# Two attention stages of a Perceiver kernel: maxima of a key block taken in four-row groups at the head, and mask and maxima of the latent attention added by products in the banks

## The chip, the cores and the metric

The kernel runs on one core of one Trainium2 chip. The metric is the device time of one execution in microseconds (us), the median of several runs. PE is the matrix engine (TensorE), DVE the vector engine, ACT the scalar engine, POOL GpSimd, SP the engine whose queue issues the transfers; a PSUM bank holds 512 float32 columns in 128 partitions.

## The reference

A two-layer model over 16 batches of 64 latent rows, width 256, with 1601 context rows a batch. Layer 0 has a cross-attention with relative embeddings, a latent (low-rank) causal self-attention and a mixture of experts; layer 1 a masked cross-attention, a delta rule and a quantised feed-forward part. The change lies in the first two. Cut to what matters:

```python
x = x + xattn(layernorm(x), ctx, ctx, ...)      # first cross-attention
#   q, k, v = x Wq + bq, ctx Wk + bk, ctx Wv + bv     16 heads of 16; 64 queries, 1601 keys
#   attn = softmax((q k^T + q rel_k[clip(k - q, -2, 2)]) / 4)
#   out  = (attn v + attn rel_v[...]) Wo + bo
x = x + latent(layernorm(x), ...)               # latent attention
#   lat = layernorm(x W_dkv) * gamma + beta ; k, v = lat W_uk, lat W_uv ; q = x W_q
#   scores = rope(q) rope(k)^T / 4, -inf above the diagonal  (64 x 64, 16 heads)
#   out = softmax(scores) v W_o
x = x + moe(...) ; x = x + xattn(..., mask) ; x = x + delta_rule(...) ; x = x + fp4_mlp(...)
```

A softmax may subtract any number near the row's maximum; both stages subtract a maximum that is found in a pass of its own.

## The kernel before

Everything lies in SBUF between stages; each engine's instructions are written out by hand in the order in which it runs them, with semaphores between engines. `cross_attention` (L185) serves both cross-attentions: the first has `rel` and no mask, the second `mask` and no `rel`. `latent_attention` (from L1052) comes between.

**Cross-attention.** A body runs once for a batch b and does two things beside each other: it attends batch b, and it prepares the keys and maxima of batch b + 1 ("ahead"). There are 17 bodies; 15 of them, b = 0 to 14, do both, in pairs (p = 0, 1), most of them in a hardware loop.

The head of a body on PE: products for the relative embeddings (L922); `key_block` 1 of the next batch (L757, block 0 was made at the end of the last body); `denominators` (L854); `key_block` 2; the transposes of the negated maxima of batch b (L946); `key_block` 3; in even batches the `output` product (L860); `project_values(0)` (L868); then `scores(0)`, which waits until DVE has multiplied the transposed maxima by `pmask` into `nmb` (L685), since each score bank begins with a product of `nmb` with ones (L897).

The loop over chunks of 128 keys, two chunks c, c + 1 a step, c = 0, 2 to 12: `scores(c)` into banks 1 to 4 (L897, L905), `maximum(SCORED[c])`, `attend_values` of the two chunks before (L885), `maximum(VALUED[c])`, `project_values(c + 2)` (L868), `maximum(PROJECTED[c])`. ACT takes the exponentials of a step in one pass (L556), DVE copies the projected values (L698).

The maxima of the next batch are approximate, from bfloat16 copies of queries and keys (`qbf`, `kbf`). A unit is `maximum(u)`: two products of 32 rows into banks 5 and 6 (L843), and one reduction of both by DVE (L675); the next unit waits for that reduction (`max_read`). Units of key block 0 have four more products for the relative embeddings (L848). `ALL` lists 4 key blocks x 4 units. `HEADED` names groups of four products into banks 1 to 4 with one reduction over four banks (`headed(j)`, L809 on PE with products on L820, L666 on DVE with the reduction on L669); the second cross-attention has three of them at the head, the first has none. `LOOPED` is what is left for the loop.

POOL, for the next batch: copies for the relative products (`qs`), then behind the reduction `ds_done` a table (`scores_table`, L418), two products into `Dxb` (L459), and the casts of the four key blocks to bfloat16 (`keys`, L435), each when ACT has written the block (L490); then four products with `kmask` (L473) for the batch attended.

DVE at the head: denominators (`rec` L654, `oN` L656), `nmb` (L685), in even batches the addition of the output to X (L664), the first value copy.

**Latent attention.** After projections, rotation and transposes a loop over 16 batches. Before the change: `scores(b)` on PE writes 8 groups of 64 x 64 scores into banks 0 to 3 (L1309). DVE's `shift(b)` adds the mask while it copies them to SBUF (`sc`, three buffers; L1219), reduces the maxima (L1225) and subtracts them (L1226). ACT takes exponentials in place (L1155). DVE's `normalise(b)` sums (L1231), takes reciprocals (L1234) and multiplies (L1235). PE transposes the result (L1329), ACT copies it (L1163), PE multiplies by the values (L1344), ACT copies that (L1169), and every second batch PE multiplies by `wo` (L1318) and DVE adds to X (L1240). The scores run up to three batches ahead.

## Time and profile before

| | us |
|---|---|
| median of 3 runs | 2667.76 |
| lowest, highest | 2666.96, 2674.25 |
| the profiled execution | 2666.93 |
| its span, first to last instruction | 2665.1 |

| engine | busy us in the span | share |
|---|---|---|
| PE | 2457.0 | 92% |
| PE weight loads (beside PE) | 1769.6 | 66% |
| DVE | 1432.5 | 54% |
| ACT | 975.5 | 37% |
| POOL | 583.1 | 22% |

The mean granted clock of PE is 0.958 of 2.4 GHz. The first cross-attention's bodies that do both things fill most of the first 814 us, the latent attention ends at 977 us. Shares are means over stages with different limits, so the two stages are read by themselves. A view by line groups instructions by engine, line and tile: busy time, mean duration in ns, and the idle time of the engine ahead of them with what ended it. The timeline gives instructions in order of time, equal neighbours merged (x count); in brackets the idle time before, and what released it. The view by stretch gives the stretch's length and then the busy us of PE, PE's loads, DVE, ACT and POOL.

### The profile page before, as it was taken

To read this page: it belongs to the slowest core of one execution; us is meant where nothing else is said; L and a number is where in the kernel's file an instruction comes from. 1 tells how busy PE (TensorE), PEld (TensorE's weight loads), DVE (VectorE), ACT (ScalarE), POOL (GpSimd) and SP (SyncE) were. 2 spreads that over 40 slices of the span, in tenths; PEclk is the share of its full clock that TensorE was granted. 3 is DMA by queue.
4 is the path that set the end of the run, shared out by engine and by line. 5 is a ranking of instruction groups with operands and counts; after the bars stand their busy time and mean duration, and the time that the engine had idled before them with its cause. 6 is when DMAs were issued, how large, how long until landed. Compare 5 with 4: busy or idle time off the path is not lost. (4 is left out here: it accounts for less than half of the span.)

```text
span 2665.1 us, 91180 instructions
## 1 busy us (share of the span) xinstructions
PE 2457.0 (92%) x41601; PEld 1769.6 (66%) x41601; DVE 1432.5 (54%) x2340; ACT 975.5 (37%) x1286; POOL 583.1 (22%) x504
## 2 busy tenths in 40 slices
PE   7999999999998878979999999999879988998798
PEld 4776776776676655736676767676567777777466
DVE  4454454454453763365555454554556666666468
ACT  2333333333333331224444444443434433332223
POOL 2424433432441203231111111211011111111000
PEclk8999999999999659989999999999899999999899
DMA  2111111111010422121111111111100000000200
GB/s 96 33 39 33 33 39 33 28 38 39 27 39 9 182 82 65 56 80 33 45 34 45 40 39 39 39 39 47 55 2 4 4 3 3 4 3 4 83 1 16
DMA packets 56728, 102.30 MB, mean 38 GB/s; under 512 B 10272, under 2 KB 49024, under 8 KB 55024
## 3 DMA queue, kind: packets, MB, share of 16 engines
q1 hardware_dynamic: 54448, 91.35, 11.1%
q8 instruction: 332, 5.44, 0.8%
q0 software_dynamic: 1904, 5.15, 0.5%
q14 instruction: 44, 0.36, 0.0%
HBM read 90.30 MB, written 9.21 MB: 37 GB/s over the span
## 5 line engine op out<-in xcount | busy, mean ns | idle before, releaser
L675 DVE TENSOR_REDUCE x_mx<-banks 128x2 f32<-128x800 f32 (+1 forms) x422 | 416.5, 990 | 385.6 <-PE banks L843 268.1
L868 PE MATMUL banks<-x_wv,x_cT 128*128 128x256 f32 (+1 forms) x1664 | 421.3, 395 | 5.1 <-DVE x_nmb L685 5.1
L757 PE MATMUL banks<-x_cT,x_wk 128*128 128x400 f32 (+1 forms) x1024 | 381.8, 515 | 7.2 <-DMA x_cT<-in_ctx 5.7
L868 PEld LDWEIGHTS banks<-x_wv,x_cT 128*128 128x128 f32 (+1 forms) x1664 | 297.8, 188 | 70.1 <-issue 11.0
L556 ACT ACTIVATE x_PT<-banks 128x2048 f32<-128x2048 f32 (+1 forms) x112 | 196.6, 1755 | 357.9 <-PE banks L905 357.9
L558 ACT ACTIVATE x_PT<-banks,x_kbs 128x1024 f32<-128x1024 f32 (+1 forms) x208 | 221.1, 1110 | 233.1 <-PE banks L905 233.1
L757 PEld LDWEIGHTS banks<-x_cT,x_wk 128*128 128x128 f32 x1024 | 187.9, 192 | 137.5 <-issue 23.3
L905 PE MATMUL banks<-x_qbd,x_kT 32*128 32x128 f32 x6656 | 246.9, 273 | 0.0
L905 PEld LDWEIGHTS banks<-x_qbd,x_kT 32*128 32x128 f32 x6656 | 242.6, 183 | 3.6
L432 POOL TENSOR_TENSOR x_kbf<-x_kT,x_mb 128x400 bf16<-128x400 f32 (+1 forms) x128 | 122.7, 961 | 556.8 <-ACT x_kT L490 556.6
L885 PE MATMUL banks<-x_PT,x_V 128*32 128x64 f32 x13312 | 233.3, 221 | 1.1 <-ACT x_PT L556 0.3
L885 PEld LDWEIGHTS banks<-x_PT,x_V 128*32 128x32 f32 x13312 | 196.6, 110 | 51.4 <-issue 48.0
L698 DVE COPY x_V<-banks 128x512 f32<-128x512 f32 (+1 forms) x224 | 144.5, 645 | 128.0 <-PE banks L868 128.0
L473 POOL TENSOR_TENSOR x_Ej<-x_PT,x_kmask 128x1024 f32<-128x1024 f32 x64 | 148.9, 2361 | 128.8 <-ACT x_PT L556 128.8
L843 PE MATMUL banks<-x_kbf,x_qbf 32*128 32x400 bf16 (+1 forms) x844 | 143.6, 339 | 12.9 <-DVE x_mx L675 3.2
L490 ACT ACTIVATE x_kT<-banks,x_bk 128x400 f32<-128x400 f32 (+1 forms) x128 | 76.0, 594 | 151.6 <-PE banks L757 151.6
L2330 PE MATMUL banks<-d_KQ,d_KB 64*64 64x64 f32 x3584 | 124.2, 220 | 7.6 <-ACT d_KB L1999 3.5
L490 ACT ACTIVATE x_kT<-banks,x_kshift 128x400 f32<-128x400 f32 (+1 forms) x128 | 76.0, 594 | 144.6 <-PE banks L757 144.6
L2330 PEld LDWEIGHTS banks<-d_KQ,d_KB 64*64 64x64 f32 x3584 | 112.6, 134 | 23.3 <-issue 23.3
L2006 ACT ACTIVATE d_Y<-banks 128x512 f32<-128x512 f32 x96 | 57.3, 597 | 177.4 <-PE banks L2330 177.4
L843 PEld LDWEIGHTS banks<-x_kbf,x_qbf 32*128 32x128 bf16 x844 | 40.5, 91 | 113.5 <-issue 63.2
L669 DVE TENSOR_REDUCE x_mx<-banks 128x4 f32<-128x1604 f32 (+1 forms) x45 | 82.1, 1825 | 58.7 <-PE banks L820 58.7
(406 smaller groups left out, 3696.2 us busy)
## 6 DMA issues: line engine op xcount, KB each, us to landing
x_cT<-in_ctx SPq DMA_DIRECT2D x96, 400.0 KB, 3.7
x_cT<-in_ctx SPq DMA_DIRECT2D x32, 401.0 KB, 3.7
e_up<-in_mo_up SPq DMA_DIRECT2D x9, 512.0 KB, 15.6
e_down<-in_mo_down SPq DMA_DIRECT2D x9, 512.0 KB, 16.4
x_mrow<-in_mask_row SPq DMA_DIRECT2D x1, 3202.0 KB, 14.3
t_w<-in_db_w SPq DMA_DIRECT2D x3, 1024.0 KB, 8.4
e_rows<-in_c_unfilled SPq DMA_DIRECT2D x1, 2967.0 KB, 13.1
e_xg<-e_rows SPq DMA_DIRECT2D x23, 129.0 KB, 2.0
```

Of the source, the lines that this page charges most:

```text
L473: pool.tensor_tensor(Ej[:, j, :].rearrange("p (h q) -> p h q", h=H), PT[:, 0, 0, :].rearrange("p (h q) -> p h q", h=H), kmask[:, j, None, ...
L490: act.activation(kT[:, 1 - p, gg, KB0[k]:KB0[k] + KBS[k]], PJ[pb][:, 0:KBS[k]], ACT.Identity, bias=kshift[:, gg, b:b + 1] if mask else bk[ ...
L556: act.activation(out, got, ACT.Exp, scale=HD ** -0.5, bias=0.0).then_inc(exp_done, n2)
L558: act.activation(out[:, :, a], got[:, :, a], ACT.Exp, scale=HD ** -0.5, bias=kbs[0:CHK[c], p, c + a:c + a + 1]).then_inc(exp_done, 1)
L675: dve.reduce_max(mx[:, H0[k]:H0[k] + 3:2, kb], g.PS[:, first:first + 2, 0:KBS[kb]], AXX).then_inc(max_read, 1)
L698: dve.tensor_copy(V[0:CHK[c], c % 6:c % 6 + n2, :, 0:HD], PJ[pb][0:CHK[c], 0:D * n2].rearrange("p (a h d) -> p a h d", a=n2, h=H)).then_in ...
L757: last = pe.matmul(PJ[pb][:, 0:KBS[k]], wk[:, c, gg, :], cT[:, (p + 1) % 2, c, KB0[k]:KB0[k] + KBS[k]], start=c == 0, stop=c == KC - 1)
L843: last = pe.matmul(g.P[first + x][:, 0:KBS[kb]], qbf[rows(r), gg, :, :].rearrange("p i q -> p (i q)"), kbf[rows(r), gg, keys], start=True, ...
L868: last = pe.matmul(PJ[pb][0:CHK[c + k], D * k:D * k + D], cT[:, p, cc, 128 * (c + k):128 * (c + k) + CHK[c + k]], wv[:, cc, :], start=cc = ...
L885: last = pe.matmul(OT[r:r + 32, S * (h // 4):S * (h // 4) + S], V[0:CHK[c], c % 6, h, :], PT[0:CHK[c], c // 2 % NPT, c % 2, S * h:S * h + ...
L905: last = pe.matmul(SC[r][0:CHK[c + a], at:at + HPT * S], kT[rows(r), p, gg, 128 * (c + a):128 * (c + a) + CHK[c + a]], qbd[rows(r), p, gg, ...
L2330: last = pe.matmul(out, lhs(E[e], hp), rhs(E[e], hp), start=k > 0 or start, stop=True, skip_group_check=True)
```

## The change

Two edits that share no code.

**First cross-attention.** `HEADED` of the first cross-attention becomes the two groups of key block 1. On PE the first comes behind `key_block` 2 and the second behind `key_block` 3; `BEHIND` holds these places for both cross-attentions, and the second one's stay as they were. DVE reduces the first group behind the denominators and ahead of `nmb`, the second behind `nmb`. POOL casts key block 0 ahead of its wait for `ds_done`, block 1 behind the small table, and blocks 2 and 3 behind the products into `Dxb`, as before. The twelve units left go to new places: all `SCORED` and `PROJECTED` slots from c = 2 on (and 0 for the first), and of the `VALUED` slots only c = 4.

**Latent attention.** A score bank now begins with a product of a bfloat16 identity with the bfloat16 mask, the scores accumulate on it, DVE reduces the negated maximum straight from the banks into a bfloat16 tile (`nmb`, two buffers), and a second set of identity products (`shift(b)`, now on PE) adds it in the bank. ACT takes the exponentials from the banks into `sc`. The two DVE passes of the mask's addition and of the subtraction are gone. The scores of a batch wait for the exponentials of the batch before (`ex_done`) instead of for the copy. The order on PE is new: shift of b + 1, scores of b + 2, an output, values of b - 1, transposes of b. The addition of the output to X comes one batch later. Two small copies on DVE make the identity and the mask bfloat16, ahead of the scaling of the latents by gamma.

```diff
-        HEADED = [(0, 0), (0, 1), (1, 0)] if mask else []
+        HEADED = [(0, 0), (0, 1), (1, 0)] if mask else [(1, 0), (1, 1)]
+        BEHIND = {0: [0], 1: [1], "shift": [2]} if mask else {2: [0], 3: [1]}
+        EARLY = 2 if mask else 0
...
+        else:
+            SCORED = {2: 1, 4: 3, 6: 6, 8: 8, 10: 10}
+            VALUED = {4: 4}
+            PROJECTED = {0: 0, 2: 2, 4: 5, 6: 7, 8: 9, 10: 11}
...
-            def keys(bank, plan, p, b):
-                for k in range(NKB):
+            def keys(bank, plan, p, b, blocks=range(NKB)):
+                for k in blocks:
...
+                        if attend:
+                            keys(bank, plan, p, b + 1, (0,))
                         pool.wait_ge(ds_done, b + 2)
                         if attend:
                             scores_table(b, p)
+                            keys(bank, plan, p, b + 1, (1,))
...
                     if attend:
-                        keys(bank, plan, p, b + 1)
+                        keys(bank, plan, p, b + 1, range(2 if rel else 0, NKB))
...
-                for j in range(ahead_of - 1):
+                for j in range(EARLY) if ahead_of else ():
                     headed(j)
                 if tail and attend:
                     denominators()
+                if ahead_of and not mask:
+                    headed(0)
...
-                    placed = range(NHD) if attend else ()
...
+                    for k in range(NKB - 1) if attend else ():
+                        if k and b:
+                            key_block(bank, plan, i, p, k)
+                        for j in BEHIND.get(k, ()):
+                            headed(j)
+                        if k == 1 and b:
                             denominators()
...
-                    if ahead and NHD:
-                        headed(2)
+                    for j in BEHIND.get("shift", ()) if ahead else ():
+                        headed(j)
                     if ahead and b:
                         key_block(bank, plan, i, p, NKB - 1)
+                    for j in BEHIND.get(NKB - 1, ()) if ahead else ():
+                        headed(j)
...
             def exponentials(b):
-                act.wait_ge(sub_done, b + 1)
-                act.activation(sc[:, b % 3, :, :], sc[:, b % 3, :, :], ACT.Exp, scale=HD ** -0.5).then_inc(ex_done, 1)
+                act.wait_ge(shifted, b + 1)
+                if b >= 3:
+                    act.wait_ge(tr_full, b - 2)
+                act.activation(sc[:, b % 3, :, :].rearrange("p (c r) k -> p r c k", c=KC),
+                               g.PS[:, 0:4, 0:2 * S].rearrange("p r (c k) -> p r c k", c=KC), ACT.Exp, scale=HD ** -0.5)\
+                   .then_inc(ex_done, 1)
...
+            dve.tensor_copy(identb[:, :], g.ident[:, :]).then_inc(masks_done, 1)
+            dve.tensor_copy(causalb[:, :], causal[:, :]).then_inc(masks_done, 1)
...
-                dve.tensor_tensor(x.rearrange("p (c r) k -> p c r k", c=KC),
-                                  g.PS[:, 0:4, 0:2 * S].rearrange("p r (c k) -> p c r k", c=KC),
-                                  causal[:, None, None, :].to_broadcast([128, KC, 4, S]), ALU.add).then_inc(s_read, 1)
...
-                done(dve.reduce_max(m[:, :], x, AXX))
-                dve.tensor_tensor(x, x, m[:, :, None].to_broadcast([128, 8, S]), ALU.subtract).then_inc(sub_done, 1)
+                if b >= 2:
+                    dve.wait_ge(shifted, b - 1)
+                dve.tensor_reduce(nmb[:, b % 2, :].rearrange("p (c r) -> p c r", c=KC),
+                                  g.PS[:, 0:4, 0:2 * S].rearrange("p r (c k) -> p c r k", c=KC), AXX, ALU.max, negate=True)\
+                   .then_inc(max_done, 1)
...
-            shift(0)
-            shift(1)
+            maximum(0)
             for b in range(B):
+                if b + 1 < B:
+                    maximum(b + 1)
                 normalise(b)
-                if b + 2 < B:
-                    shift(b + 2)
-                if b >= 2 and b % 2 == 0:
-                    add_output(b // 2 - 1)
+                if b >= 4 and b % 2 == 0:
+                    add_output(b // 2 - 2)
+            add_output(B // 2 - 2)
             add_output(B // 2 - 1)
...
             def scores(b):
                 if b >= 1:
-                    pe.wait_ge(s_read, b)
+                    pe.wait_ge(ex_done, b)
+                for r in range(4):
+                    pe.matmul(g.P[r][:, 0:2 * S], identb[:, :], causalb[:, None, :].to_broadcast([128, KC, S]),
+                              start=True, stop=False, skip_group_check=True)
...
+            def shift(b):
+                pe.wait_ge(max_done, b + 1)
+                for r in range(4):
+                    last = pe.matmul(g.P[r][:, 0:2 * S], identb[:, :],
+                                     nmb[:, b % 2, r:8:4, None].to_broadcast([128, KC, S]), start=False, stop=True, skip_group_check=True)
+                last.then_inc(shifted, 1)
...
+            for b in range(B + 1):
+                if b + 1 < B:
+                    shift(b + 1)
+                if b + 2 < B:
+                    scores(b + 2)
+                if b >= 3 and b % 2 == 1:
+                    output((b - 1) // 2 - 1)
+                if b >= 1:
+                    attend(b - 1)
+                if b < B:
+                    turned(b)
```

## Rows read from the trace of the kernel before

**Rows 1.** Stretches: start:end, us, busy us (instructions) by engine, TensorE clock, DMA

```profile
65.50:814.00 748.50, 737.58 (x12749) 525.40 (x12748) 369.60 (x465) 257.54 (x232) 280.37 (x191) 1.00 0.12 34
902.00:977.00 75.00, 54.62 (x608) 39.77 (x608) 58.93 (x104) 23.89 (x49) 0.00 (x0) 0.57 0.00 1
```

**Rows 2.** Timeline, latent loop: two additions of the output to X

```profile
944.12 0.42 DVE L1240 TENSOR_TENSOR X<-X,banks 128x256 f32<-128x256 f32 x1 [0.86 <-PE banks L1318]
952.62 0.42 DVE L1240 TENSOR_TENSOR X<-X,banks 128x256 f32<-128x256 f32 x1 [0.86 <-PE banks L1318]
```

**Rows 3.** Busy time by stretch, the last stretch before the clock rises

```profile
952.00:954.00 2.00, 2.00 (x34) 1.36 (x32) 1.31 (x4) 0.42 (x1) 0.00 (x0) 0.51 0.00 0
```

**Rows 4.** Timeline, first cross-attention: start us, us, engine, line, operation

```profile
439.99 1.10 PE L885 MATMUL banks<-x_PT,x_V 128*32 128x64 f32 x64
441.57 1.99 PE L868 MATMUL banks<-x_wv,x_cT 128*128 128x256 f32 x8
```

**Rows 5.** Timeline, second cross-attention, the same step

```profile
1441.14 1.10 PE L885 MATMUL banks<-x_PT,x_V 128*32 128x64 f32 x64
1442.17 1.99 PE L868 MATMUL banks<-x_wv,x_cT 128*128 128x256 f32 x8
```

**Rows 6.** Timeline, first cross-attention, the step of chunk 10

```profile
400.26 1.88 ACT L556 ACTIVATE x_PT<-banks 128x2048 f32<-128x2048 f32 x1 [3.25 <-PE banks L905]
403.01 0.09 PEld L843 LDWEIGHTS banks<-x_kbf,x_qbf 32*128 32x128 bf16 x2 [0.53 <-DVE x_mx L675]
```

**Rows 7.** Lines of PE, first cross-attention: busy us, mean ns | idle

```profile
L848 PE MATMUL banks<-x_rmaskb,x_Dxb 128*128 128x66 bf16 x240 | 17.7, 196 | 0.0
```

**Rows 8.** Timeline, head of a batch, second cross-attention

```profile
1421.92 0.35 PE L820 MATMUL banks<-x_kbf,x_qbf 32*128 32x400 bf16 x4
1422.20 2.95 PE L757 MATMUL banks<-x_cT,x_wk 128*128 128x400 f32 x8
1422.57 1.82 DVE L669 TENSOR_REDUCE x_mx<-banks 128x4 f32<-128x1600 f32 x1
```

**Rows 9.** Timeline, head of an odd batch, first cross-attention

```profile
413.89 3.76 POOL L459 TENSOR_TENSOR x_Dxb<-x_Ds,x_idq 128x1024 bf16<-128x1024 f32 x2
413.95 0.60 ACT L490 ACTIVATE x_kT<-banks,x_bk 128x400 f32<-128x400 f32 x1 [0.75 <-PE banks L757]
416.17 1.76 DVE L656 TENSOR_TENSOR x_oN<-x_oT,x_rec 128x256 f32<-128x256 f32 x1
416.96 0.42 PE L946 MATMUL banks<-ident,x_nm 128*32 128x128 f32 x8
417.86 0.41 DVE L685 TENSOR_TENSOR x_nmb<-banks,x_pmask 128x256 bf16<-128x256 f32 x1
419.77 1.82 PEld L868 LDWEIGHTS banks<-x_wv,x_cT 128*128 128x128 f32 x8
421.93 0.10 PEld L897 LDWEIGHTS banks<-x_nmb,x_ones 32*128 32x128 bf16 x4 [0.33 <-issue]
```

**Rows 10.** Lines of DVE and ACT, loop of the latent attention

```profile
L1219 DVE TENSOR_TENSOR l_sc<-banks,l_causal 128x512 f32<-128x512 f32 x16 | 10.9, 684 | 0.9 <-PE banks L1309 0.9
L1155 ACT ACTIVATE l_sc<-l_sc 128x512 f32<-128x512 f32 x16 | 10.1, 630 | 9.3 <-DVE l_sc L1226 9.3
```

**Rows 11.** Timeline, PE in the latent loop at the lower clock

```profile
949.77 1.11 PE L1329 MATMUL banks<-ident,l_sc 128*128 128x128 f32 x4 [0.84 <-DVE l_sc L1235]
950.67 1.91 PE L1318 MATMUL banks<-l_wo,l_oT 128*128 128x256 f32 x4
952.52 1.13 PE L1309 MATMUL banks<-l_kT,l_qb 32*128 32x64 f32 x16
953.58 0.58 PE L1344 MATMUL banks<-l_PT,l_V 128*32 128x64 f32 x16
```

**Rows 12.** Timeline, PE in the latent loop at the full clock

```profile
955.26 0.67 PE L1309 MATMUL banks<-l_kT,l_qb 32*128 32x64 f32 x16
956.01 0.43 PE L1344 MATMUL banks<-l_PT,l_V 128*32 128x64 f32 x16
```

More of the change, by code:

```diff
@@ L817, in headed @@
                             pe.wait_ge(exp_done, NCH * b)
-                    pe.wait_ge(kbf_done, KP * (NKB * (b + 1) + kb) + gg + 1)
+                    pe.wait_ge(kbf_done, KP * (NKB * (b + 1) + kb) + (gg + 1 if mask else 1))
                     for r in range(RT):
@@ L928, in body @@
                         pe.wait_ge(max_read, units(b + 1))
-                    placed = range(NHD) if attend else ()
-                    if placed:
-                        headed(0)
-                    for k in range(1, NKB - 1) if attend and b else ():
-                        key_block(bank, plan, i, p, k)
-                        if k == 1:
-                            if placed:
-                                headed(1)
+                    for k in range(NKB - 1) if attend else ():
[4 more added lines that the diff above has]
+                        if k == 1 and b:
                             denominators()
-                    if placed and not b:
-                        headed(1)
                 elif attend:
@@ L1309, in scores, with turned @@
                         last = pe.matmul(g.P[r][:, S * c:S * c + S], qb[32 * r:32 * r + 32, c, b, :],
-                                         kT[32 * r:32 * r + 32, c, S * b:S * b + S], start=True, stop=True)
+                                         kT[32 * r:32 * r + 32, c, S * b:S * b + S], start=False, stop=False, skip_group_check=True)
                 last.then_inc(s_full, 1)
-            def output(i):
-                pe.wait_ge(ot_out, 2 * i + 2)
-                if i >= 1:
-                    pe.wait_ge(x_done, i)
-                for j in range(2):
-                    last = pe.matmul(g.P[6][:, 0:D], oT[:, j, :, :].rearrange("p e q -> p (e q)"), wo[:, j, :],
-                                     start=j == 0, stop=j == 1)
-                last.then_inc(wo_full, 1)
-            for b in range(3):
-                scores(b)
-            for b in range(B):
+            def shift(b):
[4 more added lines that the diff above has]
+                last.then_inc(shifted, 1)
+            def turned(b):
                 pe.wait_ge(pn_done, b + 1)
@@ L1331, in _, with attend @@
                 last.then_inc(tr_full, 1)
-                if b >= 2 and b % 2 == 0:
-                    output(b // 2 - 1)
-                if b + 3 < B:
-                    scores(b + 3)
+            def attend(b):
                 pe.wait_ge(pt_out, b + 1)
@@ L1346, in _, with output @@
                 last.then_inc(av_full, 1)
+            def output(i):
+                pe.wait_ge(ot_out, 2 * i + 2)
+                if i >= 1:
+                    pe.wait_ge(x_done, i)
+                for j in range(2):
+                    last = pe.matmul(g.P[6][:, 0:D], oT[:, j, :, :].rearrange("p e q -> p (e q)"), wo[:, j, :],
+                                     start=j == 0, stop=j == 1)
+                last.then_inc(wo_full, 1)
+            pe.wait_ge(masks_done, 2)
+            scores(0)
+            shift(0)
+            scores(1)
+            for b in range(B + 1):
+                if b + 1 < B:
+                    shift(b + 1)
+                if b + 2 < B:
+                    scores(b + 2)
+                if b >= 3 and b % 2 == 1:
+                    output((b - 1) // 2 - 1)
[3 more added lines that the diff above has]
+                    turned(b)
             output(B // 2 - 1)
```

37 lines of the change are left out of this document (16 added, 21 removed).

## Prediction

> **What bounds the kernel now.** I read the busy time by stretch first, since the change touches two stages that have different limits, and then the order of time inside each. In the first cross-attention (65.5 to 814 us) PE is busy 737.58 of 748.50 us at a clock of 1.00, DVE half of it [rows 1]: PE bounds it, and only PE time or PE waits are worth anything there. In the latent attention's loop over batches (902 to 977 us, 75.00 us for 16 batches) DVE is busy 58.93 us and PE 54.62 at a mean clock of 0.57 [rows 1]. The two additions of an output to X stand 8.50 us apart, which is two batches, and DVE waits 0.86 us before each; in the rest of a period it goes from pass to pass [rows 2]. So DVE bounds the loop, 4.25 us a batch, and PE can run at half speed without being late. The clock rises from 1.2 to 2.4 GHz three times in this loop, each time behind a stretch like 952 to 954 us, where PE worked 2.00 of 2.00 us (output, scores and values without a gap) at a clock of 0.51 [rows 3]; the mean of 0.57 says that it soon falls again.
>
> **First cross-attention: the loop over key chunks.** Four of the sixteen two-bank maxima of the next batch leave the loop, in batches 0 to 14, so 15 times. Each step of two chunks had three slots (behind scores, values and projection); the slot behind the values goes in the steps of chunks 2, 6, 8 and 10 and stays only at 4. With that slot, the next projection starts 1.58 us after the values start [rows 4]. The second cross-attention has the same step without the slot, and there it is 1.03 us [rows 5]: 0.55 us less, about half of it product, half PE waiting for the reduction ahead. I take 0.5 for each of the four, as the steps differ a little: 2.0 us. In the step of chunk 10 PE also waits 0.53 us for a reduction ahead of the last unit; with one unit less in front this wait goes, but the scores of chunk 12 then meet the exponentials of chunk 10, 1.88 us from 400.26, so done at 402.14 against scores that now start at 403.02 [rows 6]. At most 0.8 us can leave this step, 0.5 of it is counted: 0.3 more. Against it, the unit behind the scores of chunk 4 is now one of key block 0, with four more products at 0.074 us [rows 7]: 0.3 lost. Sum: 2.0 us gained a batch. DVE has room: it loses four two-bank reductions and gets two four-bank ones of 1.82 us [rows 8].
>
> **First cross-attention: the head.** PE gets two groups of four products. In the second cross-attention such a group takes 0.28 us from its start to the next work [rows 8]: 0.56 us. Whether it waits, for an odd batch: group 0 would start at 416.96, in place of the transposes of the maxima [rows 9]. Its keys come from POOL, which now casts block 1 behind the small table and ahead of the two large products (3.76 us) [rows 9]: ACT ends block 1 at 414.55 [rows 9], and even at the price of one such product, 1.88, the cast is done at 416.43. The large products and the casts of blocks 2 and 3 come later on POOL's queue; they end near 420 and 422, and their first reader stands behind the scores of chunk 0, which start at 421.93. On DVE the four-bank reduction queues ahead of the product with pmask, for which scores(0) waits: from 417.93 (end of the normalisation that began at 416.17) 1.82 us to 419.75, then 0.41 to 420.2 [rows 8, 9]. PE needs that bank for the projection at 419.77 + 0.56 = 420.33, so it is in time by 0.1 us. Group 1 goes out at 420.05, before the projection; its reduction can start at 420.75 (0.65 behind the product, as in rows 8) and ends at 422.6, while PE wants scores(0) at 421.93 + 0.56 = 422.5: 0.1 us of waiting. In an even batch the output product lies between and covers it. Head: 0.56 + 0.1 = 0.66 us. The cover is thin: what DVE is later than this, PE waits. Net 2.0 - 0.66 = 1.34 us a batch, times 15: **20 us gained**.
>
> The normalisation just named reads two SBUF tiles and takes 1.76 us beside POOL's large product, where its size asks 0.4 (0.41 for the equally large product that reads a bank) [rows 9]. The Trainium skill (SBUF — State Buffer, Who interferes with whom) says that such a VectorE instruction and a GpSimd one exclude each other for the whole instruction. The trace agrees: 1.76 us. What it does here is a rival below.
>
> **Latent attention.** Removed on DVE: the mask's addition and the subtraction of the maximum, each 0.68 us; the maximum stays and reads banks [rows 10]. With the addition to X moved one batch back its wait of 0.86 us per two batches goes too [rows 2]: 4.25 - 1.37 - 0.43 = 2.45 us a batch for DVE. It is no longer the bound. Next is a chain through one set of banks: the scores of a batch can't be written before the exponentials of the last have read them. Chain: shift products, exponentials 0.63 [rows 10], mask and scores, maximum 0.68 [rows 10], shift. PE, in order, also runs values, transposes and every second batch the output, and stands idle while ACT reads the banks. Eight new bf16 products of 128 columns a batch: no row has them; at 66 columns four cost 0.30 [rows 7], twice the columns at most 0.59. I take 0.3 at the full clock, as the stored side is the same, and 0.5 at half.
> At 1.2 GHz a batch on PE is shift 0.5, idle 0.85 (the exponentials and the hand-overs around them), mask 0.5, scores 1.06, values 0.65, transposes 0.90, and the output 1.85 more in every second batch [rows 11]: 4.5 or 6.3 us. At 2.4 GHz it is 0.3, 0.85, 0.3, scores 0.75, values 0.43 [rows 12], transposes 0.55 and output 0.95 (half of rows 11, rounded up): 3.2 or 4.15. Batches 0 to 13 hold eight short and six long iterations; what lies around them (first batch, last normalisation, output, addition) I put at 10 us full, 13 at half. All at half: 36 + 38 + 14 = 88 us, 13 more than now; all at full: 25.6 + 24.9 + 10 = 60.5, 14.5 less. Which clock? PE at half would work four fifths of the time and seven eighths around an output, unbroken for five us, more than the stretch behind which it rose [rows 3]; at full its share is about 75 to 80%, between the 98.5% that held 1.00 and the 73% that did not [rows 1]. I let the first iterations, which have no output, run at half, and the rest at full: 6 + 3 x 4.5 + 5.3 + 5 x 3.2 + 5 x 4.15 + 7 = 68.6, or 6 less; with some chance that it is full from the start I take **8 us gained**. The two bf16 copies on DVE ahead of the loop run while PE projects the queries, and cost nothing; without that cover they cost at most two passes of the size in rows 10, 1.4.
>
> The products' price has a rule against it: the Trainium skill (TensorE: Matmul & The Clock Gate, LDWEIGHTS) gives a weight load as columns / 1.2 in ns, an estimated 107 ns for each of these eight. By it four products take 0.43 instead of 0.3, the loop gains 4 us instead of 8, and the time would be 2643. Here a product of rows 7 took 74 ns with its load beside it.
>
> **Sum.** The profiled execution took 2666.93 us (span 2665.1 and 1.8 around it), 0.8 below the median of 2667.76. 2666.9 - 20 - 8 = 2638.9, so 2639.
>
> **Rivals.**
> *Low clock in the latent loop.* PE waits for ACT once a batch, so the clock could fall each time as it does now. Then -20 + 13: 2660. Against it: the waits get shorter than now.
> *Normalisation held twice.* If POOL's two large products, now 1.7 us later, both go ahead of it, DVE's head runs 1.6 us late, and group 1, and behind it scores(0), about 1.2 us: 15 x 1.2 = 18 us of the 20 are gone: 2657. Against it: now it is done at 417.93, 0.3 after the product then running ended (413.89 + 3.76) [rows 9]. By the skill's rule too it waits for one instruction.
> *Reductions in the open (slower).* If DVE reaches both four-bank reductions only when PE stands before scores(0), their 3.64 us replace the 0.66: 1.64 us lost a batch, 25 in all, and with 8 gained elsewhere 2684. It decides against the change from 1.9 us of waiting a batch on (1.34 + 8/15). Against it: the times above, which leave 0.1.
> *It doesn't shorten the steps.* If the slot behind the values hid other PE work, only the head's cost is left: 15 x 0.66 = +10, -8: 2669.
>
> **How the numbers follow.** Forecast 0.70 (2625 to 2652), low clock 0.11, normalisation 0.08, slots that hide 0.06, reductions in the open 0.05. The range to 2657 leaves out the last two and part of the low clock. A measurement here can tell 0.3%, 8 us. Faster by more: 0.70 + 0.08 + a little of the low clock, 0.80; within: 0.14; slower: 0.06.
>
> **What would show it.** Projections 1.0 instead of 1.6 us behind the values in the steps of chunks 6 and 8; DVE's first four-bank reduction ahead of 418 and no wait of PE before scores(0) over 0.3 us; in the latent loop DVE no longer busy throughout, PE's longest wait for the exponentials, clock above 0.8. A clock under 0.7 there, or PE waiting over 1 us for a reduction in the head, makes it wrong.

## The result, and the profile after

The changed kernel takes 2651.0 us (median of 7 executions, 2646.53 to 2661.14) against 2665.82 us (7 executions, 2661.19 to 2674.25) for the kernel before: a ratio of 0.995, with a 95% interval of 0.9936 to 0.9965. That is 9 to 17 us less, where 28 were forecast. Timed again in a later comparison (e5 below) it took 2644.57 against 2667.77 us, a ratio of 0.992 (0.9898 to 0.9941). The direction held, and 2651 lies inside the forecast's 2625 to 2652; but that band is wide, and the gain of 14.8 and 23.2 us by the two pairs of medians is about half and four fifths of the 28.

The execution that was profiled is the slowest of the seven, 2661.14 us at a mean granted clock of 0.956; a second profile of the same kernel (e5), 2645.59 us, had 0.964. Executions of one kernel differ here by some 15 us, and the longer ones have the lower mean clock. The code behind the latent loop, the same in both kernels, took 1688.1 us in the profile before, 1691.6 after and 1679.4 in e5. So totals of single profiles are not compared below; stages are.

The stretches of the profile after that answer to [rows 1] (start:end, us, busy us (instructions) of PE, weight loads, DVE, ACT and POOL, TensorE clock, DMA): steady bodies of the first cross-attention, and the latent loop, cut where its clock rises.

```profile
110.00:750.00 640.00, 636.42 (x10936) 455.76 (x10936) 314.94 (x378) 223.70 (x205) 248.37 (x168) 1.00 0.13 35
893.60:940.50 46.90, 38.61 (x393) 28.75 (x392) 21.29 (x40) 11.16 (x24) 0.00 (x0) 0.53 0.00 1
940.50:967.70 27.20, 20.83 (x340) 15.26 (x340) 16.46 (x32) 10.87 (x25) 0.00 (x0) 1.00 0.01 2
```

The first cross-attention is bound by PE as before (99% busy). In the loop DVE is no longer the bound, as forecast: 37.75 of 74.1 us where it was 58.93 of 75.00 [rows 1]. And yet the loop is only 0.9 us shorter, because some 44 of the 74.1 us ran at the lower clock (a mean of 0.53 over the first 46.9).

What the changed stages gave in this execution, stage by stage, by the starts of the same products in both traces (body D to D: from the products with x_Rd of one body to those of the next):

| stage | before, us | after, us | change | forecast |
| --- | --- | --- | --- | --- |
| first body with attention | 48.6 | 51.9 | +3.3 | -1.3 |
| each steady body, even / odd batch's head | 51.71 / 49.98 | 50.63 / 49.07 | -1.08 / -0.91 | -1.34 |
| 13 steady bodies | 660.1 | 648.2 | -11.9 | -17.4 |
| latent loop | 75.0 | 74.1 | -0.9 | -8 |

These sum to -9.5 us, some -10.5 with the last such body at the price of a steady one. The loop was up to 8 us shorter in other executions (e2, e11 below), so the rows give a gain of some 10 to 18 us, where the medians gave 14.8 and 23.2.

The steps inside a steady body, from the start of one pair of chunks' scores to the next, medians:

| from scores of chunk | 0 | 2 | 4 | 6 | 8 | 10 | 12, and head, odd / even |
| --- | --- | --- | --- | --- | --- | --- | --- |
| before | 5.84 | 5.63 | 4.88 | 5.23 | 5.13 | 4.36 | 18.91 / 20.65 |
| after | 5.84 | 5.12 | 5.12 | 4.66 | 4.76 | 3.74 | 19.84 / 21.41 |
| change | 0 | -0.51 | +0.24 | -0.57 | -0.37 | -0.62 | +0.93 / +0.76 |
| forecast | 0 | -0.5 | +0.3 | -0.5 | -0.5 | -0.8 | +0.66 (mean) |

The step of chunk 6 in the timeline (start us, us, engine, line, operation), the answer to [rows 4]:

```profile
439.86 1.10 PE L896 MATMUL banks<-x_PT,x_V 128*32 128x64 f32 x64
440.89 1.99 PE L879 MATMUL banks<-x_wv,x_cT 128*128 128x256 f32 x8
```

The projection starts 1.03 us behind the values, as in the second cross-attention [rows 5], no longer 1.58 [rows 4]. The head of an odd batch, the answer to [rows 9], on PE, its weight loads (PEld), DVE and POOL:

```profile
413.42 2.85 PE L768 MATMUL banks<-x_cT,x_wk 128*128 128x400 f32 x8
416.20 0.35 PE L831 MATMUL banks<-x_kbf,x_qbf 32*128 32x400 bf16 x4
416.48 0.43 PE L953 MATMUL banks<-ident,x_nm 128*32 128x128 f32 x8
416.83 2.95 PE L768 MATMUL banks<-x_cT,x_wk 128*128 128x400 f32 x8
419.72 0.35 PE L831 MATMUL banks<-x_kbf,x_qbf 32*128 32x400 bf16 x4
420.00 1.99 PE L879 MATMUL banks<-x_wv,x_cT 128*128 128x256 f32 x8
...
422.06 0.13 PEld L908 LDWEIGHTS banks<-x_nmb,x_ones 32*128 32x128 bf16 x4 [0.47 <-issue]
...
415.41 1.50 DVE L665 TENSOR_TENSOR x_oN<-x_oT,x_rec 128x256 f32<-128x256 f32 x1
416.83 1.81 DVE L678 TENSOR_REDUCE x_mx<-banks 128x4 f32<-128x1600 f32 x1
418.56 0.41 DVE L696 TENSOR_TENSOR x_nmb<-banks,x_pmask 128x256 bf16<-128x256 f32 x1
420.12 1.83 DVE L678 TENSOR_REDUCE x_mx<-banks 128x4 f32<-128x1600 f32 x1 [1.15 <-PE banks L831]
...
414.72 3.94 POOL L468 TENSOR_TENSOR x_Dxb<-x_Ds,x_idq 128x1024 bf16<-128x1024 f32 x2
```

Group 0 goes out at 416.20 without a wait, 0.28 us ahead of the next products. The normalisation (oN) ended at 416.91, close to where the first of POOL's two large products did (half of 3.94 behind 414.72 is 416.69): it waited for one of them, not for both. Group 1's reduction ends at 421.95, and scores(0), which needs those banks, starts at 422.09, 2.09 us behind V's projection; it was 1.82 before (420.11 to 421.93), and in e10 below, where nothing is waited for, it is 1.83. The last key block and the projection behind it, in the kernel before:

```profile
417.32 2.95 PE L757 MATMUL banks<-x_cT,x_wk 128*128 128x400 f32 x8
420.11 1.89 PE L868 MATMUL banks<-x_wv,x_cT 128*128 128x256 f32 x8
```

### The profile page after: what moved, and what is told of

It is laid out like the page before. It is cut to its first block and busy times, and to the rows that moved or that the text cites. A ratio compares the mean times of both kernels' runs of the same rounds, so it can differ in the third digit from the quotient of the medians.

```text
span 2659.4 us, 91403 instructions
## 1 busy us (share of the span) xinstructions
PE 2458.6 (92%) x41729; PEld 1776.8 (67%) x41729; DVE 1401.4 (53%) x2280; ACT 974.7 (37%) x1286; POOL 584.9 (22%) x504
## 5 line engine op out<-in xcount | busy, mean ns | idle before, releaser
L684 DVE TENSOR_REDUCE x_mx<-banks 128x2 f32<-128x800 f32 (+1 forms) x362 | 357.0, 990 | 420.2 <-PE banks L854 293.2
L879 PEld LDWEIGHTS banks<-x_wv,x_cT 128*128 128x128 f32 (+1 forms) x1664 | 296.5, 188 | 66.1 <-DVE x_nmb L696 5.8
L678 DVE TENSOR_REDUCE x_mx<-banks 128x4 f32<-128x1600 f32 (+1 forms) x75 | 136.7, 1823 | 78.6 <-PE banks L831 78.6
L2365 PE MATMUL banks<-d_KQ,d_KB 64*64 64x64 f32 x3584 | 128.5, 224 | 10.3 <-issue 5.4
L854 PE MATMUL banks<-x_kbf,x_qbf 32*128 32x400 bf16 (+1 forms) x724 | 123.2, 340 | 6.4 <-POOL x_Dxb L468 3.0
L441 POOL CAST x_kbf<-x_kT 128x802 bf16<-128x802 f32 (+1 forms) x64 | 54.7, 856 | 329.7 <-ACT x_kT L499 312.0
```

The lines of the kernel that those rows point to most:

```text
L678: dve.reduce_max(mx[:, gg::2, kb], g.PS[:, 1:1 + RT, 0:KBS[kb]], AXX).then_inc(head_read, 1)
L684: dve.reduce_max(mx[:, H0[k]:H0[k] + 3:2, kb], g.PS[:, first:first + 2, 0:KBS[kb]], AXX).then_inc(max_read, 1)
L879: last = pe.matmul(PJ[pb][0:CHK[c + k], D * k:D * k + D], cT[:, p, cc, 128 * (c + k):128 * (c + k) + CHK[c + k]], wv[:, cc, :], start=cc = ...
L2365: last = pe.matmul(out, lhs(E[e], hp), rhs(E[e], hp), start=k > 0 or start, stop=True, skip_group_check=True)
```

## What the first body did

The body that makes batch 0's attention and batch 1's maxima, on PE and on POOL, after the change:

```profile
57.95 0.97 PE L933 MATMUL banks<-x_Rd,x_qs 128*128 128x32 f32 x8
65.40 0.52 PE L831 MATMUL banks<-x_kbf,x_qbf 32*128 32x400 bf16 x4 [6.48 <-POOL x_kbf L441]
65.85 0.66 PE L953 MATMUL banks<-ident,x_nm 128*32 128x128 f32 x8
67.86 0.52 PE L831 MATMUL banks<-x_kbf,x_qbf 32*128 32x400 bf16 x4 [1.34 <-DVE x_mx L678]
...
62.55 1.91 POOL L424 TENSOR_TENSOR x_Dx<-x_Ds,x_idq 128x1024 f32<-128x1024 f32 x1 [5.05 <-DVE x_Ds L659]
64.40 0.85 POOL L441 CAST x_kbf<-x_kT 128x800 bf16<-128x800 f32 x1
```

Here all key blocks were made a body earlier, so PE has nothing but short products ahead of group 0. POOL casts block 1 only behind the small table, the table waits 5.05 us for DVE's Ds, and PE stands 6.48 us for the cast. The transposes of the maxima, and scores(0) behind them, queue up behind group 0. The prediction worked the head out for a steady odd batch and multiplied by fifteen.

## What the latent loop did

Its iterations at the lower clock (first three rows: mask, scores, values of one iteration; the next mask 4.42 us later) and at the full clock:

```profile
908.19 0.61 PE L1321 MATMUL banks<-l_causalb,l_identb 128*128 128x128 bf16 x4 [0.69 <-ACT l_sc L1169]
908.73 1.13 PE L1325 MATMUL banks<-l_kT,l_qb 32*128 32x64 f32 x16
909.79 0.66 PE L1354 MATMUL banks<-l_PT,l_V 128*32 128x64 f32 x16
912.61 0.61 PE L1321 MATMUL banks<-l_causalb,l_identb 128*128 128x128 bf16 x4 [0.69 <-ACT l_sc L1169]
...
943.64 0.40 PE L1321 MATMUL banks<-l_causalb,l_identb 128*128 128x128 bf16 x4 [0.69 <-ACT l_sc L1169]
943.96 0.67 PE L1325 MATMUL banks<-l_kT,l_qb 32*128 32x64 f32 x16
946.87 0.41 DVE L1253 TENSOR_TENSOR X<-X,banks 128x256 f32<-128x256 f32 x1
947.56 0.40 PE L1321 MATMUL banks<-l_causalb,l_identb 128*128 128x128 bf16 x4 [0.69 <-ACT l_sc L1169]
950.47 0.40 PE L1321 MATMUL banks<-l_causalb,l_identb 128*128 128x128 bf16 x4 [0.69 <-ACT l_sc L1169]
```

The maximum, in the same stretch, and the exponentials, the answer to [rows 10]:

```profile
907.54 0.60 ACT L1169 ACTIVATE l_sc<-banks 128x512 f32<-128x512 f32 x1 [1.17 <-PE banks L1332]
909.93 0.69 DVE L1237 TENSOR_REDUCE l_nmb<-banks 128x8 bf16<-128x512 f32 x1 [2.17 <-PE banks L1325]
```

The exponentials take 0.60 us from the banks, 0.63 from SBUF before [rows 10]. An iteration without an output takes 4.42 us at half clock and 2.91 at full (947.56 to 950.47), one with an output 6.43 and 3.92 (943.64 to 947.56). The forecast had 4.5 and 3.2, 6.3 and 4.15: the prices were right within 0.3. The wait for the exponentials is 0.69 us whatever the clock, and the addition to X waits no more, where it had waited 0.86 us [rows 2]. What was wrong is which iterations get which price: the forecast let three without an output run at half, and one with an output in part (its 5.3); here it was the run-in (the first turns, up to 903.8 us) and seven whole iterations, three of them with an output (the mask at 903.77 to the mask at 940.73).

## Experiments

Two theories stood at the start. **Theory 1**: the first cross-attention brought nearly all of the gain, and the latent part next to nothing, since the clock stays low in its loop. **Theory 2**: the latent part is worth its 8 us as a rule, and the shortfall is in the first cross-attention.

**e1 and e2: one part each.** e1 has the changed first cross-attention and the latent attention of before, e2 the reverse.

> The first cross-attention's part alone, with the latent attention as in the kernel before. Theory A (the latent part brought next to nothing because the clock stayed low in its loop): this kernel has nearly the whole gain, 11 to 15 us less than the kernel before: 15 bodies at 0.9 to 1.1 us each, less some 3 us lost once where the first batch's second key block is cast late. Rival B (the latent part is worth its forecast 8 us in most executions, and the profiled one was an exception): 4 to 7 us less. In the profile, D to D periods in the steady bodies 49.1 and 50.6 us, the first one 51.9.

> The latent attention's part alone, the cross-attentions as in the kernel before. Theory A: the loop's first 40 to 45 us run at 0.5, the loop takes 72 to 76 us instead of 75.0, and the kernel is 0 to 3 us faster than the one before. Rival B: the clock rises within some 20 us, the loop takes 64 to 69 us, and the kernel is 6 to 11 us faster.

Measured: e1 2654.41 us, a ratio of 0.9958 (0.9938 to 0.9979), 6 to 17 us less; steady bodies of 49.1 and 50.7 us (medians), the first one 51.9, the loop 74.5. The interval takes in both theories' forecasts (11 to 15, 4 to 7), so this time decides nothing. e2 2654.21 us, a ratio of 0.9971 (0.9958 to 0.9985), 4 to 11 us less; its loop took 66.1 us:

```profile
901.20:925.20 24.00, 18.92 (x204) 14.10 (x201) 11.84 (x22) 5.01 (x10) 0.00 (x0) 0.50 0.01 1
925.20:967.40 42.20, 32.57 (x535) 24.06 (x532) 25.92 (x51) 17.02 (x38) 0.00 (x0) 1.00 0.01 2
```

The same loop, here at half clock for 24 us and not for 44, is 8.9 us shorter than before: the forecast's 8. Theory 1 falls for this execution; theory 2 does not explain the 74.1 us either. New theory: the length of the low stretch differs from one execution to the next.

**e5, e11 and e12: the same kernels profiled again.** e5 and e11 are the changed kernel, e12 the kernel of e2.

> The changed kernel once more, as it is, for a second profile and more times. Theory A (in the changed kernel the low clock in the latent loop lasts differently from one execution to the next): the loop takes 66 us again in some executions, as it did with the latent part alone, and the times lie in two groups some 8 us apart, about 2648 and 2657. Rival B (the first part brings the loop to a point where the clock always stays low for 44 us): the loop takes 74 us again, and the times stay above 2650. Either way the first D to D period is 51.9 us.

> A third look at the changed kernel as it is. If the length of the low stretch in the latent loop goes by what the kernel did before the loop, it is some 44 us and the loop takes 74 us, as in the two looks so far. If it goes by the execution, 66 us is as likely.

> A second look at the kernel with the latent part alone. If the length of the low stretch goes by what the kernel did before the loop, it is some 24 us and the loop takes 66 us, as in the first look at this kernel. If it goes by the execution, 74 us is as likely.

Measured: e5 2644.57 us (six executions, 2640.07 to 2652.93), with a loop of 74.1 us in the profile; e11 2643.7 us, loop 70.2; e12 2657.47 us, loop 66.1. The low and the full stretch of e5, then of e11:

```profile
890.30:936.70 46.40, 38.56 (x394) 28.77 (x392) 21.27 (x40) 10.73 (x23) 0.00 (x0) 0.52 0.00 1
936.70:964.50 27.80, 20.90 (x341) 15.25 (x340) 16.49 (x32) 11.28 (x25) 0.00 (x0) 1.00 0.01 2
```

```profile
890.70:926.60 35.90, 29.22 (x302) 21.75 (x300) 16.60 (x31) 8.19 (x18) 0.00 (x0) 0.52 0.01 1
926.60:960.90 34.30, 26.29 (x432) 19.34 (x432) 21.17 (x41) 13.83 (x31) 0.00 (x0) 1.00 0.01 2
```

One kernel gave 74.1, 74.1 and 70.2 us, so the length does differ between executions; the two profiles of e2's kernel gave 66.1 both times, so what precedes the loop may count too. Of the runs below, e3 and e9 have the same loop as well and gave 66.1, e10 74.2. Each further pair of iterations at half clock costs 4 us (10.85 against 6.84), so the three lengths are one pair apart. Of e5's theories neither held whole: the loop took 74 us again, but the times above 2650 that this rival demanded are not there (four of the six are below), nor are the two groups of the other.

The rise itself has a place. In all ten traces in which the loop goes through a long low stretch, it comes in a stretch of unbroken PE work around an output, or within 0.5 us of its end. In the profile after it comes at 940.4 us:

```profile
935.00:940.00 5.00, 5.00 (x44) 3.59 (x44) 2.51 (x5) 0.28 (x1) 0.00 (x0) 0.50 0.00 0
```

But it need not come at the first of them: 912.6 to 918.3 us was as unbroken and passed at 0.50, and so did the next. It came at the third here and in e5 and e10, at the second in e11, at the first in the other six.

**e3: the late cast.** The change with one edit, on GpSimd, in the first body only:

```
-                            keys(bank, plan, p, b + 1, (0,))
+                            keys(bank, plan, p, b + 1, (0,) if later(b) else (0, 1))
                         pool.wait_ge(ds_done, b + 2)
                             scores_table(b, p)
-                            keys(bank, plan, p, b + 1, (1,))
+                            keys(bank, plan, p, b + 1, (1,) if later(b) else ())
```

> The whole change, with GpSimd's casts of key blocks 0 and 1 for batch 1 (the first body with attention alone) put ahead of its wait for the table; the other bodies as they were. Theory A (order on GpSimd costs the first body 3.3 us, since the block's cast stands behind a table that is late there): the first D to D period goes from 51.9 back to 48 to 49.5 us, and the kernel is 2 to 4 us below the changed kernel's 2651, 16 to 18 us below the one before. Rival B (it is the low clock in that body, not the cast): the wait of 6.5 us ahead of the headed product goes, but the period stays above 51 us.

Measured: 2640.27 us, a ratio of 0.9921 (0.9903 to 0.9939), 16 to 26 us less than before, and a first body of 47.5 us. PE and POOL in that body:

```profile
55.24 0.97 PE L933 MATMUL banks<-x_Rd,x_qs 128*128 128x32 f32 x8
59.09 0.52 PE L831 MATMUL banks<-x_kbf,x_qbf 32*128 32x400 bf16 x4 [2.88 <-issue]
...
53.93 1.66 POOL L441 CAST x_kbf<-x_kT 128x802 bf16<-128x802 f32 x2 [15.10 <-ACT x_kT L499]
```

The casts are done at 55.6 and group 0 starts 3.85 us behind the products with x_Rd, not 7.45. The body goes from +3.3 to -1.1 against before: GpSimd's order, not the clock, had cost it. The low clock is still there in that body (group 0 takes 0.52 us for 0.35). How much it regains depends on the execution: with the same edit e6 and e7 took 48.3 and 48.6 us, and the body without the change took 48.6, 47.7 (e2) and 47.9 (e12). So the loss is given back, 3.3 to 4.4 us; a gain like a steady body's is not shown. The whole time is 10.7 and 4.3 us below the two medians of the changed kernel; the loop took 66.1 us in this execution, so the body's own rows, and not the total, tell what the edit is worth.

**e4: the loop's order.** TensorE's and ScalarE's order in the loop over b:

```
-shift(b+1); scores(b+2); output; attend(b-1); turned(b)
+shift(b+1); output; attend(b-1); scores(b+2); turned(b)
 ...
-exponentials(b+1); copy of PT(b-1); copy of oT(b-1)
+copy of PT(b-1); exponentials(b+1); copy of oT(b-1)
```

> The whole change, with the latent loop's order on TensorE set to shift(b+1), output, values(b-1), scores(b+2), transposes(b), and ScalarE's copy of the transposed weights put ahead of the next exponentials, so that values stand where TensorE waited 0.69 us for the exponentials and the transposes where it waits for the maxima. Theory A (the idle gaps hold the clock at 0.5): the clock rises within 15 us of the loop's start, an iteration costs 2.9 to 3.9 us, the loop 55 to 63 us, the kernel 11 to 18 us below the changed one. Rival B (the clock in the loop does not go by these gaps): it stays at 0.5 for some 35 to 45 us, an iteration costs 3.7 and 5.7 us at half, the loop 62 to 70 us, the kernel 5 to 11 us below the changed one. Rival C (ScalarE or VectorE takes over as the bound): the loop stays above 70 us.

Measured: 2640.25 us, a ratio of 0.9916 (0.99 to 0.9932), the loop 60.4 us:

```profile
894.20:913.80 19.60, 16.07 (x182) 11.97 (x180) 9.40 (x17) 5.01 (x10) 0.00 (x0) 0.56 0.01 2
913.80:954.60 40.80, 34.76 (x564) 24.41 (x556) 28.14 (x55) 17.73 (x38) 0.00 (x0) 1.00 0.01 2
```

```profile
PE banks L1333 <- DVE l_nmb L1238: 4.2, 13, 0.8
PE banks L1322 <- ACT l_sc L1169: 2.4, 7, 0.7
```

The second fence is the table of PE's waits in this loop (us in total, times, longest): the changed kernel had 10.3 us in 15 waits for the exponentials. A pair of iterations costs 6.34 us at full clock where the change has 6.84, and the clock rose after 20 us. The loop is as short as theory A expected, though the clock rose later than its 15 us, and the shorter iterations are shown. Whether the clock rose earlier because the gaps are fewer is not: 24 us was to be had with them, and in both orders it rose at the first output, which stands 17.3 us behind the loop's start here and 21.3 in e2.

**e6, e7 and e8: does the loop's entry decide?** e6 is e3 and e4 together. e7 adds to e6, and e8 to the changed kernel alone, 28 products that nobody reads, where TensorE waits ahead of the loop and in its first turns:

```
+def filler(k, times):
+    for _ in range(times):
+        pe.matmul(g.P[k][:, :], identb[:, :], causalb[:, None, :].to_broadcast([128, 8, S]), start=True, stop=True, skip_group_check=True)
+# 5 ahead of the last two groups of transposes, 4 behind them (bank 0); then in bank 7:
 scores(0); +filler(7, 3); shift(0); +filler(7, 3); scores(1); +filler(7, 3)
+# b = 0 and 1: 3 behind shift(b+1); b = 0: 4 behind scores(2)
```

> The whole change with both earlier edits: the casts of key blocks 0 and 1 early in the first body, and the latent loop in the order shift, output, values, scores, transposes. If the two act on different stages, their gains add: the first D to D period 47.5 us, the loop 58 to 62 us, the kernel 2630 to 2637, 28 to 34 us below the kernel before, so some 4 us below either edit alone. Rival: the low clock that the faster stage leaves elsewhere takes half of it back, and it stays at 2637 to 2641.

> As the kernel with both edits, and 28 products of 128 rows by 128x512 bf16 into banks that nobody reads, put where TensorE waits just ahead of the latent loop and in its first three batches (9 ahead of the first scores, 9 between the first scores and shifts, 10 in the first two turns). At 0.21 us each at full clock they fit the waits. Theory A (the clock falls at the loop's start since TensorE has little to do there, and once it is full the loop's own work keeps it): no low stretch between the loop's start and its end, loop 51 to 56 us, the kernel 4 to 9 us below the one with both edits. Rival B (the loop's own products, of 32 rows or 32 columns, let the clock fall again): a low stretch of 10 us or more returns after the last filler, loop 58 us or more, kernel same or slower.

> The changed kernel with the same 28 fillers and nothing else (the loop's order as the change has it, with 0.69 us gaps). Theory A (the clock at the loop's entry decides, not its gaps): no low stretch in the loop, each pair of iterations 6.8 us throughout, loop 55 to 59 us, the kernel 8 to 14 us below the changed one. Rival B (the gaps of 0.69 us pull the clock down again): low stretches return, the loop takes 64 us or more.

Measured: e6 2634.72 us, ratio 0.9884 (0.9861 to 0.9907), first body 48.3 us, loop 60.1, so the two gains add as expected. e7 2630.22 us, ratio 0.9862 (0.9841 to 0.9883), loop 56.1. e8 2637.22 us, ratio 0.9887 (0.9865 to 0.9909), loop 59.2. The whole loop in one row, e8 first, then e7:

```profile
895.50:954.70 59.20, 47.95 (x752) 33.81 (x751) 37.77 (x72) 22.02 (x48) 0.00 (x0) 1.00 0.01 2
```

```profile
889.40:945.60 56.20, 49.16 (x753) 33.32 (x751) 37.59 (x72) 22.86 (x48) 0.00 (x0) 1.00 0.01 2
```

In e8 the waits of 0.69 us stand as in the changed kernel:

```profile
907.19 0.40 PE L1331 MATMUL banks<-l_causalb,l_identb 128*128 128x128 bf16 x4 [0.69 <-ACT l_sc L1169]
```

The last filler is done by some 904.3, and the clock is 1.00 to the end of the loop. So these gaps don't pull a full clock down: a loop that leaves its run-in at 1.00 stays there, while one whose clock falls there stays at 0.50 for 17 to 44 us. In the changed kernel the clock was 0.78 from 893.6 to 898 us and 0.50 from there, so it fell in the run-in, where PE was busy 2.73 of 4.40 us between the first maxima and exponentials:

```profile
893.60:898.00 4.40, 2.73 (x41) 2.03 (x40) 0.79 (x2) 0.60 (x1) 0.00 (x0) 0.78 0.02 4
```

In all ten traces of the loop without fillers the clock fell within 3 us of the loop's start, in both with fillers it did not. e8's loop is 14.9 us shorter than e5's beside it, its median only 7 us lower: in the two profiles, e8's body ahead of the first one with attention took 4.1 us more (27.1 for 23.0) and the code behind the loop 2.8, code that the two kernels share. e7 is the best kernel of this study, 31 to 42 us below the one before.

**e9 and e10: the head.** e9 leaves one headed group and puts the other's two units back, into chunks 2 and 6 (the slot behind the values is free in chunks 8 and 10 only). e10 puts each group between the two halves of its key block and, on DVE, the first reduction ahead of the normalisation:

```
 e9: HEADED = [(1, 0)], BEHIND = {2: [0]}, VALUED = {2: 2, 4: 5, 6: 8}
 e10: key_block(..., k, (0,)); headed(j); key_block(..., k, (1,)), for k = 2 and 3; EARLY = 1
```

> The whole change with one of the two headed groups only (the second group's two units go back into chunks 2 and 4 to 6, so units are taken out of chunks 8 and 10 alone, and one product of 0.28 us stands at the head). Theory A (every slot taken out is worth its own time and the groups cost what they take on TensorE): chunks 8 and 10 are 0.35 to 0.65 us shorter each, chunk 4 no longer than in the kernel before, the head and tail 0.3 to 0.5 us longer, a body 0.4 to 0.7 us shorter than before, that is about half of the whole change's 0.9 to 1.1. Rival B (the second group's wait at the end of the head is what ate the gain): a body is as short as or shorter than with both groups, 0.9 us or more below before.

> The whole change, with each headed group put between the two halves of its key block instead of behind it, and the first reduction ahead of the normalisation on VectorE. Theory A (in every second body the first scores wait some 0.2 us for the second reduction, which makes the head 0.93 us longer instead of 0.76): the double bodies' longer tail comes down to 0.7 to 0.8 us over before, a double body 0.15 to 0.3 us shorter, and no wait ahead of the first scores. Rival B (the groups now wait for the cast or for the first reduction): a wait of 0.2 us or more appears ahead of a headed product and the body is as long or longer.

Measured: e9 2645.88 us, ratio 0.9931 (0.991 to 0.9953); e10 2649.03 us, one execution. In e9 the step of chunk 6 is 0.11 shorter than before, those of chunks 8 and 10 0.37 and 0.62, and tail and head 0.28 longer in odd and even batches alike: 0.82 us a body. So one group has most of the gain of two, neither the half of theory A nor the 0.9 or more of rival B. The first group costs its products, 0.28 us, the second 0.48 in even and 0.65 in odd batches. In e10's odd head:

```profile
415.63 1.61 PE L766 MATMUL banks<-x_cT,x_wk 128*128 128x400 f32 x4
417.17 0.35 PE L829 MATMUL banks<-x_kbf,x_qbf 32*128 32x400 bf16 x4
417.45 1.61 PE L766 MATMUL banks<-x_cT,x_wk 128*128 128x400 f32 x4
418.89 1.89 PE L877 MATMUL banks<-x_wv,x_cT 128*128 128x256 f32 x8
420.72 0.40 PE L906 MATMUL banks<-x_nmb,x_ones 32*128 32x512 bf16 x4
```

Scores now follow the projection at 1.83 us, without the wait. But block 3, cut in two, takes 3.26 us with its group (415.63 to 418.89), 0.19 more than the block's 2.79 before the change and the group's 0.28 together; block 2, cut in the same way (411.95 to 415.27), costs 0.26 more; and the body is 0.1 (odd) to 0.3 us (even) longer than with the whole change. Theory A was right on the wait and wrong on the gain: the cure costs at least what it saves.

## Why the prediction was right or wrong

The direction held, and so did the steps and DVE's release in the loop; the size did not, and three of its terms were wrong: the head's 0.66 us, the factor 15, and which iterations of the loop run at half clock. Against the forecast they are worth some 5 us, 4.6, and 7.1 in the profiled execution (2.6 as a mean of the eight traces with this loop).

- **What bounds each stage** was right: PE in the first cross-attention, DVE in the loop before, and DVE no longer after.
- **The steps**: -1.83 us a batch, forecast -2.0. Four slots at 0.5 were near (0.51, 0.57, 0.37, 0.62), the unit of block 0 at chunk 4 too (+0.24 for 0.3). The extra 0.3 in chunk 10 came to 0.1.
- **The head**: +0.76 and +0.93, forecast 0.66. The wait of the odd batch was put at 0.1 and is 0.26 (2.09 for 1.83 behind the projection). In both, the key block ahead of group 1 takes 2.89 us to the next work (416.83 to 419.72) where it took 2.79; and in the even batch, where the output product follows the group, that one takes 1.83 us to the projection's start for 1.73. So odd 0.56 + 0.26 + 0.1, even 0.56 + 0.1 + 0.1. The 0.28 us of [rows 8] is a group between the transposes of the maxima and a key block, and was put at the other place without a row for it. With the steps that makes -0.91 to -1.08 a batch for -1.34: 5 us of the shortfall over 15.
- **"Times 15"** is the step that failed first. Batch 0's body has neither the key blocks that gave POOL its time nor an early Ds; it lost 3.3 us where 1.3 were to be gained, 4.6 of the shortfall, and e3 gives it back with one edit.
- **"I let the first iterations, which have no output, run at half, and the rest at full"** is the other. The prices of an iteration at either clock were within 0.3 us, and the whole loop at full clock took 59.2 us in e8 (forecast 60.5). Four of the eight traces with this loop and no fillers (e2, e3, e9, e12) ran as the sum has it, at half up to the first output: 66.1 us, 8.9 less than before (forecast 8). In the other four the stretch around the first output passed at 0.50, and the loop took 70.2 to 74.2 us; over the eight the gain is 5.4. So what failed is that the rise was taken as settled there. It was argued from PE's share of work, more of it meaning a higher clock, and the profiled execution shows a share of 38.61 in 46.90 us, 82%, held at 0.5, and 20.83 in 27.20, 77%, held at 1.00: share doesn't tell the two apart. What the runs show in its place is that the clock of the run-in is kept at 1.00 where fillers hold it there (e7, e8), and that after a fall it rises at the first, second or third output, at 4 us for each one missed. The low clock was given as a rival, with 88 us if it held throughout (its terms, with 13 us around the iterations, add to 87); it held for some 44 us of 74.
- **The price of the bf16 products**: 0.3 us for four at full clock was right. From the mask's start to the scores' it is 0.32 (943.64 to 943.96), 0.54 at half. By the estimate of 107 ns a load from the Trainium skill (TensorE: Matmul & The Clock Gate, LDWEIGHTS) it would have been 0.43; the trace does not agree, with 0.23 us for four loads at full clock, 58 ns each. That the prediction's 2643 for that price lies near the 2644.57 of e5 is luck: the loop's clock and the first body made the difference.
- **The rivals**: the normalisation held twice did not happen. It took 1.50 us beside POOL's products and ended 0.2 us behind the end of the first, estimated as half of the two. The Trainium skill (SBUF — State Buffer, Who interferes with whom) has such a VectorE instruction and a GpSimd one exclude each other for the whole instruction; the trace agrees, 1.50 us where 0.4 was put by size. Reductions in the open did not happen either (0.26 us of waiting, from 1.9 on it would have decided), nor slots that hide.
- **The signs**: projections at 1.03 us, the first reduction at 416.83, 0.26 us ahead of scores(0) and the exponentials as PE's longest wait in the loop (10.3 us in all) came as named. The loop's mean clock was 0.70, not above 0.8, and in the first body PE waited 1.34 us for a reduction, one of the two signs of being wrong.

Open: why the clock rises at the first, second or third of the unbroken stretches, after 24, 34 or 44 us of the same work, and how much of it what precedes the loop decides. What the two bf16 copies ahead of the loop cost is not told apart from the clock either: from the first product of the latent attention to the first scores it took 38.2 us before, 39.3 after and 37.9 in e5.

## What to carry to other kernels

A price per iteration worked out for a steady body must be worked out again for the first and the last one, above all the order of the queues: there the early work that covers a moved step is missing. Where a loop can run at either clock, its entry is to be looked at, not only its share of work: some products that nobody reads, placed where TensorE waits anyway, were worth 4 to 15 us of the loop here, and 4 to 7 us of the kernel's median. Of an edit that adds two equal things, the second may cost about twice the first (0.48 and 0.65 us for 0.28), so each is priced where it stands.

## What the runs showed of the hardware

The same loop, with the same gaps of 0.69 us, stayed at a granted clock of 0.50 for 24, 34 or 44 us before it rose; at 1.00 it stayed to its end, over 50 us in e8, though PE's share of work was the higher one at 0.50 (82% for 77%). A group of four bf16 products between two fp32 blocks costs 0.28 us beside the transposes of the maxima, and 0.48 between a key block and an output product: 0.1 more on either side. A key block of eight products cut in two by such a group costs 0.19 to 0.26 us more than block and group (e10).
